# Second attention with scores from stacks of three bf16 parts, computed twice

## The reference, cut to what matters

```python
q = (x @ Wq).reshape(b, n, N_HEADS, HEAD_DIM)          # 32 heads of 8
k, v = jnp.split(ctx @ Wkv, 2, axis=-1)
q = apply_axial_rope(q, pos_map)
k = apply_axial_rope(k, ctx_pos_map)
logits = jnp.einsum('bqhd,bkhd->bhqk', q, k) * scale
w = jax.nn.softmax(logits, axis=-1)
attn = jnp.einsum('bhqk,bkhd->bqhd', w, v)
return attn.reshape(b, n, N_HEADS * HEAD_DIM) @ Wout + bout
```

## Time and profile before

| | us |
|---|---|
| median of 3 runs | 2450.47 (2449.96 to 2451.26) |
| profiled execution | 2454.56 |
| its span in the profile | 2452.8 |
| TensorE busy in the span | 2116.2 (86%) |
| VectorE, ScalarE, GpSimd busy | 1286.8, 1130.7, 966.8 |

### The profile page before, as it was taken

The page is one execution under the profiler, slowest core; times in us unless marked ns, Lnnn a source line. Parts: engine busy times, 40 slices in busy tenths (PEclk is TensorE's granted clock), DMA queues, the critical chain, the costliest instruction groups (busy, mean ns, idle before and its releaser), DMA issues.

```text
span 2452.8 us, 37314 instructions
## 1 busy us (share of the span) xinstructions
PE 2116.2 (86%) x11277; PEld 1472.7 (60%) x11277; DVE 1286.8 (52%) x3478; ACT 1130.7 (46%) x3509; POOL 966.8 (39%) x879
## 2 busy tenths in 40 slices
PE   6999999869999987978999999987999677884682
PEld 4666666846666664645666656644666456663672
DVE  2545545466667554345555555434333577884233
ACT  4444444345555554335566555432333266762230
POOL 1212211024343444543444545322555411557574
PEclk8999999989999998989999999999999889997896
DMA  9999500200000032650000000044566514324698
GB/s 352 358 351 345 158 1 1 70 1 1 1 19 3 17 90 51 102 147 1 1 1 1 26 12 30 10 145 126 90 103 103 119 31 110 105 84 121 152 183 192
DMA packets 223565, 233.92 MB, mean 95 GB/s; under 512 B 35803, under 2 KB 215267, under 8 KB 222604
## 3 DMA queue, kind: packets, MB, share of 16 engines
q1 hardware_dynamic: 186124, 183.40, 25.0%
q0 software_dynamic: 37248, 48.14, 10.9%
HBM read 95.60 MB, written 143.85 MB: 98 GB/s over the span
## 4 chain that ended last, share of the span: by engine, by line
PE 30%; DVE 8%; issue 6%; DMA 4%; ACT 3%; POOL 3%; SPq 1%; POOLq 0%; DVEq 0%; ACTq 0%
PE ps L129 25%; ACT work L2613 1%; DMA moe_sum<-xn,work 1%; DMA moe_sum<-work 1%; PE ps L604 1%; PE ps L578 1%; DVE n_negm L2701 1%; PE ps L1891 1%; DMA work<-f_rows 1%; PE ps L1906 1%; POOL moe_sum L3110 1%; POOL f_rows L3013 1%; PE ps L430 1%; ACT work L659 1%; POOL rk L461 0%
## 5 line engine op out<-in xcount | busy, mean ns | idle before, releaser
L129 PE MATMUL ps<-weights,work 128*128 128x126 f32 (+6 forms) x3188 | 622.2, 330 | 22.6 <-ACT weights L2622 19.2
L129 PEld LDWEIGHTS ps<-weights,work 128*128 128x128 f32 (+2 forms) x3188 | 447.4, 194 | 73.8 <-issue 33.6
L129 PE MATMUL ps<-work,weights 128*128 128x512 f32 (+3 forms) x1408 | 481.4, 466 | 3.1 <-ACT work L668 3.1
L129 PE MATMUL ps<-xn_T,weights 128*128 128x512 f32 (+5 forms) x960 | 361.2, 510 | 19.4 <-DVE qvar L723 8.0
L129 PEld LDWEIGHTS ps<-work,weights 128*128 128x128 f32 (+2 forms) x1408 | 213.7, 186 | 86.1 <-issue 74.8
L1969 POOL DMA_INDIRECT f_sum<-work x120 | 185.3, 1544 | 182.8 <-ACT work L1930 148.6
L743 POOL TENSOR_TENSOR work<-work,rinv 128x512 f32<-128x512 f32 x128 | 133.4, 1042 | 300.6 <-DVE rinv L694 278.5
L129 PEld LDWEIGHTS ps<-xn_T,weights 128*128 128x128 f32 (+3 forms) x960 | 151.0, 191 | 116.6 <-issue 95.8
L1037 POOL TENSOR_TENSOR work<-weights,head_sel 128x512 f32<-128x512 f32 x128 | 134.9, 1058 | 203.7 <-PE ps L129 178.5
L988 ACT ACTIVATE work<-ps,n_negm 128x128 f32<-128x128 f32 x512 | 145.6, 374 | 116.5 <-DVE n_negm L1014 112.8
L3013 POOL DMA_INDIRECT f_rows<-ctx,weights x128 | 126.7, 990 | 147.7 <-DVEq L3102 99.5
(11 more groups left out here) (332 smaller groups left out, 3534.3 us busy)
## 6 DMA issues: line engine op xcount, KB each, us to landing
f_rows<-weights SPq DMA_DIRECT2D x25, 2176.0 KB, 19.6
work<-f_rows SPq DMA_DIRECT2D x120, 136.0 KB, 2.5
weights<-in_L_ffn_gate_up_proj SPq DMA_DIRECT2D x29, 384.0 KB, 4.6
f_rows<-weights SPq DMA_DIRECT2D x4, 2592.0 KB, 25.7
work<-f_rows SPq DMA_DIRECT2D x64, 162.0 KB, 3.7
f_sum<-weights SPq DMA_DIRECT2D x4, 2176.0 KB, 16.5
weights<-in_L_ffn_W SPq DMA_DIRECT2D x96, 88.0 KB
moe_sum<-weights SPq DMA_DIRECT2D x3, 2176.0 KB, 18.0
```

The costliest lines, as they stand in the source:

```text
L129: return nc.tensor.matmul(out, lhsT, rhs, start=start, stop=stop, skip_group_check=True)
```

## The change

What it does:
- Each query and key after the rope is split on GpSimd into three bf16 parts that add up to the fp32 value (`split_pool`), written by SP to DRAM and read back as stacks (`stacks_sp`): a head's stack has 3 x 3 x 8 = 72 rows, in which each part of the query stands against each part of the key, so that one bf16 product of 72 rows is the sum of all nine. A unit is 16 heads of one batch (4 steps); there are four slots for units. In a half there are 16 writes and 4 x 8 reads.
- Scores are computed with tokens on partitions (four products into `S_PAIR`), only for the maximum. The negated maxima of a step (128 x 4) are turned by TensorE to 4 x 128, split into a high bf16 part (ScalarE) and a low one (VectorE), and one step later scores are computed a second time with keys on partitions (`T_PAIR`), each product followed by one with `l1_pick` that adds the maximum's two parts to all 128 partitions.
- ScalarE makes one exponential of 512 columns from that bank, into what V's product reads. The turns of the probabilities, their copies, the key blocks and the fp32 score product go.
- The angles of the next body come two to a step (12 to 14), its sines at 15, its first rope at 16 to 18, V at 20 and 21; the router's steps move from 16 to 29 to 22 to 30.
- Some semaphores are shared with other stages, and GpSimd makes other constants.

The diff, cut:

```diff
@@ -880,20 +882,29 @@
...
+        def stacks(self, u, j):
+            slot = l1_slots[u % self.n // NB % len(l1_slots)]
+            head = u % NB * NB + j
+            return slot[:, 0, head, :], slot[:, 1, head, :]
     P_LAG = 3
...
     OUT_AT = O_LAG + 1
-    KB_RING, KB_AHEAD = 4, 3
-    s_kblk = tile(WK, 3072, KB_RING * W).rearrange("p (n h k) -> p n h k", n=KB_RING, h=NB)
+    TURN_LAG, TWIN_LAG = 1, 2
+    S_PAIR, T_PAIR = (B4, B5), (B6, B3)
+    PARTS = 3
+    STACK = PARTS * PARTS * 8
+    LOW = 32
     n_on = tile(WK, 5120, 512).rearrange("p (n d) -> p n d", n=2)
...
-    def slim_pe(pe, S, q_t, v_flat, o_t, beside):
+    def slim_pe(pe, S, v_flat, o_t, beside):
         A, s = S.A, S.s
...
@@ -905,23 +916,22 @@
...
             if S.new:
-                c, r, b, hf = place(A, t)
-                done(pe, A.kblk_ready, s, t)
-                before = t - 3 if t >= 3 else max(i for i in range(A.n - 3, A.n) if i % 3 == t) - A.n
-                done(pe, A.p_ready, s, before)
-                mm(S_BANKS[t % 3], q_t[:, hf, b * P:(b + 1) * P],
-                   s_kblk[:, t % KB_RING, :, :].rearrange("p h k -> p (h k)")).then_inc(A.s_mm.sem, 1)
-            u = t - P_LAG
+                if t % NB == 0:
+                    unit = t // NB
+                    done(pe, stack_in[unit % 4], 2 * s + unit // 4, 127)
+                done(pe, A.m_low, s, t - 2)
+                for j in range(NB):
+                    q, k = A.stacks(t, j)
+                    last = mm(S_PAIR[t % 2][:, j * P:(j + 1) * P], q, k)
+                last.then_inc(A.s_mm.sem, 1)
+            u = t - TURN_LAG
             if S.has(u):
-                done(pe, A.p_ready, s, u)
-                done(pe, A.pt_ready, s, u - 1)
-                for j in range(NB):
-                    last = nc.tensor.transpose(B6[:, j * P:(j + 1) * P], n_p[:, u % 4, j, :], ident[:])
-                last.then_inc(A.pt_tr.sem, 1)
+                done(pe, A.negm_ready, s, u)
+                nc.tensor.transpose(S_PAIR[u % 2][0:NB, 0:P], n_negm[:, u % 4, 0:NB], ident[:]).then_inc(A.m_tr.sem, 1)
             u = t - PV_LAG
...
                 blk, g = u // A.groups, u % A.groups
-                done(pe, A.pt_ready, s, u)
+                done(pe, A.p_ready, s, u)
                 if u in A.needs_v:
...
@@ -933,6 +943,16 @@
...
                 last.then_inc(A.o_mm.sem, 1)
+            u = t - TWIN_LAG
+            if S.has(u):
+                done(pe, A.m_low, s, u)
+                done(pe, A.p_ready, s, u - 2)
+                for j in range(NB):
+                    q, k = A.stacks(u, j)
+                    bank = T_PAIR[u % 2][:, j * P:(j + 1) * P]
+                    mm(bank, k, q, True, False)
+                    last = mm(bank, l1_pick[:, j, :], l1_low[:, u % 2, :], False, True)
+                last.then_inc(A.twin_mm.sem, 1)
             u = t - O_LAG
...
@@ -975,19 +995,16 @@
...
             turned(t - O_LAG - 1)
-            u = t - P_LAG
-            if u % 2 == 0 and S.has(u):
-                done(act, A.pt_tr, s, u)
+            u = t - TURN_LAG
+            if S.has(u):
+                done(act, A.m_tr, s, u)
+                done(act, A.twin_mm, s, u - 2)
+                nc.scalar.activation(l1_low[0:NB, u % 2, :], S_PAIR[u % 2][0:NB, 0:P], ACT.Copy).then_inc(A.m_high.sem, 1)
+            u = t - TWIN_LAG
+            if S.has(u):
+                done(act, A.twin_mm, s, u)
                 done(act, A.o_mm, s, u - 2)
-                nc.scalar.activation(n_pt[:, u % 2, :], B6, ACT.Copy).then_inc(A.pt_ready.sem, 1)
-            if S.new:
-                i = t % 4
-                done(act, A.negm_ready, s, t)
-                done(act, A.pt_tr, s, t - 4)
-                for j in range(NB):
-                    last = nc.scalar.activation(n_p[:, i, j, :], S_BANKS[t % 3][:, j * P:(j + 1) * P], ACT.Exp,
-                                                bias=n_negm[:, i, j:j + 1])
-                last.then_inc(A.p_ready.sem, 1)
+                nc.scalar.activation(n_pt[:, u % 2, :], T_PAIR[u % 2], ACT.Exp).then_inc(A.p_ready.sem, 1)
             if S.tail and t - A.tail_t in (4, 5):
...
@@ -1010,14 +1027,14 @@
...
                 done(dve, A.s_mm, s, t)
-                done(dve, A.p_ready, s, t - 4)
-                nc.vector.tensor_reduce(n_negm[:, t % 4, 0:NB], S_BANKS[t % 3].rearrange("p (h k) -> p h k", h=NB), AX.X, ALU.max,
+                done(dve, A.m_tr, s, t - 4)
+                nc.vector.tensor_reduce(n_negm[:, t % 4, 0:NB], S_PAIR[t % 2].rearrange("p (h k) -> p h k", h=NB), AX.X, ALU.max,
                                         negate=True).then_inc(A.negm_ready.sem, 1)
-            u = t - P_LAG
-            if u % 2 and S.has(u):
-                done(dve, A.pt_tr, s, u)
-                done(dve, A.o_mm, s, u - 2)
-                nc.vector.tensor_copy(n_pt[:, u % 2, :], B6).then_inc(A.pt_ready.sem, 1)
+            u = t - TURN_LAG
+            if S.has(u):
+                done(dve, A.m_high, s, u)
+                nc.vector.tensor_tensor(l1_low[LOW:LOW + NB, u % 2, :], S_PAIR[u % 2][0:NB, 0:P], l1_low[0:NB, u % 2, :], ALU.subtract)\
+                    .then_inc(A.m_low.sem, 1)
             if S.tail and t - A.tail_t in (0, 1):
...
@@ -1026,27 +1043,9 @@
...
-    def slim_pool(pool, S, k_t, head_sel, beside):
+    def slim_pool(pool, S, beside):
         A, s = S.A, S.s
-        def key_block(body, g):
-            c, r, b, hf = place(A, g)
-            if g in A.needs_qk:
-                done(pool, A.needs_qk[g][0], body, A.needs_qk[g][1])
-            done(pool, A.s_mm, body, g - KB_RING)
-            nc.gpsimd.tensor_tensor(out=s_kblk[:, g % KB_RING, :, :],
-                                    in0=k_t[:, hf, b * P:(b + 1) * P].unsqueeze(1).broadcast_to([P, NB, P]),
-                                    in1=head_sel[:, r, :].unsqueeze(2).broadcast_to([P, NB, P]),
-                                    op=ALU.mult).then_inc(A.kblk_ready.sem, 1)
-        if S.new and not S.old:
-            for g in range(KB_AHEAD):
-                key_block(s, g)
         for t in S.steps:
-            if S.new and t + KB_AHEAD < A.n:
-                key_block(s, t + KB_AHEAD)
-            elif S.new and S.ahead:
-                key_block(s + 1, t + KB_AHEAD - A.n)
             if S.tail and t - A.tail_t == 2:
...
@@ -1190,6 +1193,53 @@
...
+    def split_pool(pool, body, j):
+        link = Chain(pool, L1.split_chain, body, 6 * j)
+        done(pool, parts_out, 2 * body + j - 1, 255)
+        x = [z[:, :, j * CW:(j + 1) * CW].rearrange("p f (b c) -> p b f c", b=CB) for z in (l1_q, l1_k)]
+        rest = [z.rearrange("p (b f) c -> p b f c", b=CB) for z in l1_rest]
+        parts = [[z[:, :, a, :].rearrange("p (b f) c -> p b f c", b=CB) for a in range(PARTS)] for z in l1_parts]
+        for i in range(2):
+            done(pool, rope_ready, body, 2 * j + i)
+            link(nc.gpsimd.tensor_copy(parts[i][0], x[i]))
+            link(nc.gpsimd.tensor_tensor(out=rest[i], in0=x[i], in1=parts[i][0], op=ALU.subtract))
+            link(nc.gpsimd.tensor_copy(parts[i][1], rest[i]))
+            nc.gpsimd.tensor_tensor(out=parts[i][2], in0=rest[i], in1=parts[i][1], op=ALU.subtract).then_inc(L1.split_ready.sem, 1)
+    def rope_pool(pool):
+        def beside(S, t):
+            if S.new and t == 2:
+                split_pool(pool, S.s, 1)
+            if S.ahead and t == 17:
+                split_pool(pool, S.s + 1, 0)
+            early_pool(pool, S, t)
+        split_pool(pool, 0, 0)
+        return beside
+    STACK_RUNS = [(0, turn, 0, PARTS) for turn in range(PARTS)] + [(1, 0, 0, PARTS)]
+    STACK_RUNS += [(1, turn, a, n) for turn in (1, 2) for a, n in ((turn, PARTS - turn), (0, turn))]
+    def stacks_sp(sp):
+        for half in range(2 * NS):
+            body, j = half // 2, half % 2
+            for i in range(2):
+                done(sp, L1.split_ready, body, 2 * j + i)
+                for x in range(2):
+                    for r in range(4):
+                        sp.dma_start(parts_dram[half, i, :, :, 4 * x + r, :, :].rearrange("u a h c -> h u a c"),
+                                     l1_parts[i][64 * x + r:64 * x + 64:4, :, :, :]).then_inc(parts_out.sem, 16)
+            done(sp, parts_out, half, 255)
+            for unit in range(4):
+                if half >= 1:
+                    done(sp, L1.twin_mm, (half - 1) // 2, (half - 1) % 2 * 16 + unit * NB + NB - 1)
+                part = parts_dram[half, :, unit].rearrange("i a r h c -> i a r (h c)")
+                for i, turn, first, n in STACK_RUNS:
+                    row = 8 * (PARTS * turn + (first if i == 0 else (first - turn) % PARTS))
+                    sp.dma_start(l1_slots[unit][row:row + 8 * n, i, :, :].rearrange("p h c -> p (h c)"),
+                                 part[i, first:first + n].rearrange("a r c -> (a r) c")).then_inc(stack_in[unit].sem, 16)
...
@@ -1203,13 +1253,11 @@
...
                 rope_angles_pe(pe, S.s + 1)
```

(45 more changed lines are left out.)

59 lines of the change are left out of this document (32 added, 27 removed).

## The result

The changed kernel takes 2544.17 us (median of 4 runs, 2541.86 to 2547.81), the kernel before 2450.86 us (4 runs, 2449.96 to 2452.4). The ratio is 1.0365, with an interval from 1.0345 to 1.0385: slower by 93 us, outside the range given. The profiled execution took 2546.34 us, 91.8 more than that of before.

A forecast was written before the change was run, and what follows sets the result against it. TensorE was taken to bound the second attention: 215 (steps) + 60 (side work) + 7.5 (low clock) + 77.6 (stalls) + 15 (start) = 375 us against 378, so 2447 us in all; own range 2436 to 2457, overall 2424 to 2468.

The forecast's parts named there:

- The pairs: TensorE's steady step in the second attention: each bf16 load and product pair taken at 56 ns, at most 81 ns.
- Rival 2: TensorE's bf16 pairs cost 81 instead of 56 ns, the load being unhidden: 18 us more, 2465 us; chance 0.20.
- low clock, kept as before: Second attention: TensorE's loss to the granted clock of 0.98 stays 7.5 us; uncertainty up to 8 us more.
- granted clock under 0.95 through the stage: Sign in the second attention that would show the forecast wrong; four more clock dips were priced at 13 us.
- The stalls: Second attention: side tasks, mostly VectorE's, stall TensorE 77.6 us over four bodies, against 30 idle before.
- rival 1: Second attention: more slack, stalls 55 and not 78 us, sum 22 us lower, 2425 us; chance 0.30.
- The start: Start of the second attention: splits, writes and reads before the first stacks make the first scores 15 us late.
- rival 3: Supply of stacks late: writes 8 us more, splits twice 3.4 us; 11 us more at the start (2458); chance 0.13.
- The sum: Second attention: steps, side work, low clock, stalls and start make 375 us against 378, 3 us less.
- the first term: TensorE's 128 steady steps in the second attention at 1.68 us: 215 us, 65 us less than before.

## Why the prediction was wrong

**The pairs** are the step that failed, at the bound "From above: if nothing of the load hides, a pair is 26 + 55 = 81 ns." The 26 ns of the earlier trace rows are the distance in a train of equal loads, not the duration of one that stands alone. Where the number of rows changes between small and large, a pair takes 158 ns: the load (0.09 to 0.10 us in the timeline after) and the products seem to take their turns. With 128 rows beside 72 a load starts with the product before it (624.51 and 624.51, PEld and PE); in the changed kernel it starts 0.14 us behind that (621.13 and 620.99). Rows at half clock fit this too:

```profile
547.74 0.10 PEld L129 LDWEIGHTS ps<-work 72*128 72x128 bf16 x1
547.75 0.29 PE L129 MATMUL ps<-work 72*128 72x128 bf16 x1
547.97 0.29 PE L129 MATMUL ps<-weights 36*128 36x128 bf16 x1
549.07 0.61 PE L129 MATMUL ps<-work 72*128 72x128 bf16 x4
549.47 0.42 PE L930 MATMUL ps<-ident,n_negm 128*4 128x128 f32 x1
```

An alternating pair takes 0.22 us there and an equal one 0.10 to 0.11: the product has doubled, while the surcharge is 0.1 us as at full clock, and the load's row is as long as there. Why a change of rows brings it about, no run shows. The trace of before had the better rows, which I did not use: weight loads (PEld) with their own mean (count, busy us, mean ns), here that of the turns and that of the bf16 loads of the earlier trace rows.

```profile
L919 PEld LDWEIGHTS ps<-ident,work 128*128 128x128 f32 x512 | 63.2, 143 | 92.4 <-issue 82.3 <-ACT work L988 9.8
L129 PEld LDWEIGHTS ps<-weights 128*128 128x128 bf16 x42 | 1.5, 96 | 0.0
```

55 + 143 = 198 ns would have been a bound that holds the measured 158, and 55 + 96 = 151 ns, from loads of the same type and size, comes near it. The Trainium skill ("TensorE: Matmul & The Clock Gate", LDWEIGHTS (loading the stationary operand)) gives a load by its columns over 1.2 in ns, 107 for 128 of them; with the 56 of the product that is an estimate of 163 for a load that nothing hides, and the trace agrees within 5 ns (158), though its rows give the load 90 to 100 ns and not 107. For equal rows the value of 56 ns was right (56 measured, and 58 with 72 and 128 in turn). That the fp32 turns stream their columns twice, from which the 55 came, no row of before shows. The other figure of that page (Back-to-back issue gap), 81 ns for sustained pairs at 128 columns, was seen in none of these runs: equal rows run faster, and small and large in turn twice as slow. Cost: 8 changes in a step, 2.51 - 1.68 = 0.83 us, x 128 = 106 us.

Rival 2 had the direction, dearer bf16 pairs, but neither the size nor the cause. Its sum was 2465; with 158 for 81 ns in 8 of 12 pairs it would have been well above 2500. The row count of the picks (36) stood in the diff, and the rows that I had read had no weights of under 64 rows beside such of over 64. The trace of before has some, though, in this very stage (fp32, the product for the rope's angles with weights of 2 rows):

```profile
639.18 0.60 PE L207 MATMUL ps<-ident,y_T 128*128 128x128 f32 x4
639.71 1.12 PE L129 MATMUL ps<-weights,freq 2*128 2x512 f32 x2
640.76 1.13 PE L129 MATMUL ps<-work,weights 128*128 128x512 f32 x2
641.73 0.49 PE L919 MATMUL ps<-ident,work 128*128 128x128 f32 x3
```

Four turns take 0.53 us up to the small weights, where they take 0.44 in the earlier trace rows; the small product takes 1.05 and the score product behind it 0.97, where two passes of 512 columns take 0.86. So a surcharge of 0.1 us at a change between small and large could be read before the change was made, and these rows, not those of equal weights, were the ones to price 72 rows against 36.

**The clock** was "low clock, kept as before", 7.5 us. It is 0.84 in place of 0.99. At half clock a step of the changed kernel lasts 4.11 us (545.36 to 549.47, the turn in the rows above) against 2.51, so a microsecond there does 0.61 of the work; with a clock of 0.86 over the 450 us from 530 to 980, 126 us are at half clock, of which 39% are lost: 49 us, as the runs with V twice gave. In the earlier trace rows the dip of the kernel before is 0.11 x 30 / 0.5 = 6.6 us long; the changed kernel stayed down for 20 us above, and in its other profile (the chip with 2600.4) for 37, in which TensorE's row has only 1 us of gaps:

```profile
541.50:578.50 37.00, 35.88 (x180) 26.34 (x181) 13.74 (x29) 7.55 (x18) 7.06 (x8) 0.50 0.25 61
```

Even with equal rows, 0.93 and not 0.98 remained. The line "granted clock under 0.95 through the stage" was in the list of what would show the forecast wrong, priced at 13 us.

**The stalls** were 17.4 us and not 77.6, but because TensorE was slower: a step of 2.51 hides tasks which one of 1.68 does not. With equal rows they were 52.9 and 52.5, which is not the forecast but rival 1's 55, in the places named: rope, angles with statistics, router. Spreading the angles took 14 of them away. So the mechanism was right and the forecast's size half too high. The likely reason, which no run tests: the side tasks were taken as each alone, with no credit for what TensorE's side work in neighbouring steps gives.

**The start** was 19.15 us against 15. The split operations took 0.61 and 1.15 us as put (0.61 and 1.04), the k split ended at 518.8 (517 forecast), unit 0 was there at 532.5 (528.3 forecast). The 16 writes were issued in 10.70 us, 0.67 each, where I took 0.43 and named 0.91 as the other end. That is rival 3's price, 4 of its 8 us; its condition, a supply that falls behind later, never came: there is no other wait for stacks in the stage.

**The sum.** For the stage without the start I had 360 us against 378, 18 less; it was 71 more. 106 (pairs) + 42 (clock, 49 - 7.5) - 60 (stalls) = 88, and 88 - 18 = 70; with the start that is the 90 us by which the stage ends later. With the first term mended, the kernel with 72 rows, the forecast of 2447 us stands beside 2444.05 and 2445.89: the two terms that were off there, stalls (25 too many) and clock (0.93: 0.07 x 359 - 7.5, about 18 more), mostly cancel, and the start took 3 more. That this sum came out is in part luck.

What stays open: why the clock is 0.93 with equal rows and 0.99 before. TensorE has more gaps there (297 us busy of 350, before 325), but the changed kernel with 334 busy has only 0.84, and the kernel without picks, 288 busy, 0.88; doubling the V products changed both, the gaps and what lies between them, and nothing was run that changes one alone.

## What to carry to other kernels

Look at the number of rows of neighbouring matmuls' weights: if a small tile (36 or 64 rows here) stands between large ones (72, 128), pad it with zero rows to the large size, which cost nothing (56 ns a pair) where the alternation cost 0.1 us at each change. A price worked out from rows holds for their shape only; an operation in a shape or a sequence that no row read so far has needs a search of the whole trace for a like one (here the product with weights of 2 rows), and failing that a wide bound, upward above all. And when work on the bounding engine shrinks, count anew the stalls that it hid and the clock that it kept.

## What the runs showed of the hardware

- Pairs of a 128-column load and 128 columns of bf16: 56 ns with 72 rows throughout, 58 with 72 and 128 in turn, 158 with 72 and 36, 160 with 72 and 64. One change between small and large costs 0.1 us; a train of small ones costs no more than one of large ones (four of 36 rows, with the picks behind the key products). The kernel before shows a like surcharge in fp32 at weights of 2 rows (0.09 to 0.19 us in each of three places).
- TensorE can stand at half clock without a gap in its row of busy times (685 to 705 us, 20.00 of 20.00 busy by its modelled rows, 0.50). Adding 114 us of matmuls to that stage lengthened it by 49.7.
- A write of 48 KB from 16 partitions in runs of 256 bytes kept SP's queue for 0.67 us (16 in 10.70), where a plain issue took 0.44, at a DMA share of 0.33; two queues doubled the share (0.68) and ended the writes 3.6 us earlier, yet the first stacks came 1 us earlier only.
